# A decoder layer on one core: the order of the instructions on four engines from the first load to the last slot

## Time and profile before

| what | us |
|---|---|
| median of 3 runs | 340.77 (340.64 to 340.9) |
| the profiled execution's own time | 340.39 |
| its span, first to last instruction | 338.6 |
| TensorE matmuls busy | 281.4 |
| VectorE busy | 225.5 |
| ScalarE busy | 229.3 |
| GpSimd busy | 192.3 |

### The profile page before, as it was taken

How to read it: one execution, slowest core, us unless ns; L and a number is a source line. 1 busy time by engine, 2 the same in 40 slices (tenths; PEclk the granted TensorE clock), 3 DMA queues, 4 the chain that set the end, 5 groups by cost and what they waited for, 6 DMA issues and landing times.

```text
span 338.6 us, 5747 instructions
## 1 busy us (share of the span) xinstructions
PE 281.4 (83%) x1518; PEld 213.2 (63%) x1518; DVE 225.5 (67%) x488; ACT 229.3 (68%) x456; POOL 192.3 (57%) x381
## 2 busy tenths in 40 slices
PE   1366747586689899999999999899999999999950
PEld 1253524244366587777878877667888888878740
DVE  2789999999897869977686777363533454443420
ACT  3788788899578759987787787466454564544740
POOL 2436775768847656865755746647425343255571
PEclk9999787859599999999999999999999999999995
DMA  7999981978492792004002202303211021010000
GB/s 241 389 387 387 225 196 62 180 124 161 127 214 98 127 185 66 1 31 158 0 33 93 66 0 89 100 0 129 91 63 33 32 94 62 3 58 30 24 8 6
DMA packets 17407, 37.02 MB, mean 109 GB/s; under 512 B 1504, under 2 KB 1632, under 8 KB 17377
## 3 DMA queue, kind: packets, MB, share of 16 engines
q0 software_dynamic: 6496, 15.74, 19.5%
q1 hardware_dynamic: 10880, 20.92, 19.2%
HBM read 26.68 MB, written 10.76 MB: 111 GB/s over the span
## 4 chain that ended last, share of the span: by engine, by line
PE 62%; ACT 7%; issue 5%; DVE 5%; POOL 3%; DMA 2%; POOLq 0%; ACTq 0%; DVEq 0%; SPq 0%
PE bank_z L1589 5%; PE bank_y L1589 5%; PE bank_z L1590 5%; PE bank_z L1593 5%; PE bank_y L1590 5%; PE bank_y L1593 5%; PE bank_m L1589 4%; PE bank_m L1593 4%; PE bank_m L1590 4%; PE bank_tr L1558 4%; PE bank_c L1491 3%; PE bank_q L1558 2%; PE bank_a L1491 1%; PE bank_m L1553 1%; PE bank_a L1558 1%
## 5 line engine op out<-in xcount | busy, mean ns | idle before, releaser
L353 POOL TENSOR_TENSOR x<-x,bias_b 128x512 f32<-128x512 f32 x19 | 24.6, 1293 | 25.9 <-PE bank_q L1558 25.8
L1589 PE MATMUL bank_y<-c_hi,h_hi 128*128 x76 | 31.5, 415 | 1.6 <-ACT h_hi L650 1.4
L1589 PE MATMUL bank_m<-f_hi,m_hi 128*128 128x512 f32 x76 | 31.5, 415 | 1.6 <-ACT m_hi L650 1.6
L1589 PE MATMUL bank_z<-c_hi,a_hi 128*128 x76 | 30.8, 406 | 2.1 <-issue 1.4
L358 POOL DMA_INDIRECT out<-r,token_of x19 | 20.2, 1063 | 18.6 <-ACT r L689 11.7
L1590 PE MATMUL bank_m<-f_lo,m_hi 128*128 128x512 f32 x76 | 30.1, 396 | 0.0
L1590 PE MATMUL bank_z<-c_lo,a_hi 128*128 x76 | 30.1, 396 | 0.0
L1590 PE MATMUL bank_y<-c_lo,h_hi 128*128 x76 | 30.1, 396 | 0.0
L313 POOL TENSOR_TENSOR n_d<-n_v,minus_half 128x1 f32<-128x1 f32 (+1 forms) x46 | 27.0, 586 | 3.8
L1090 DVE TENSOR_TENSOR act_z<-bank_z,act_z 128x512 f32<-128x512 f32 x19 | 13.1, 688 | 22.0 <-ACT act_z L664 22.0
L312 POOL TENSOR_SCALAR n_v<-n_dev 128x1 f32<-128x1 f32 (+1 forms) x46 | 8.7, 190 | 33.2 <-ACT rows L669 19.7
(11 more groups left out here) (205 smaller groups left out, 855.4 us busy)
## 6 DMA issues: line engine op xcount, KB each, us to landing
f_sum<-in_factors POOLq DMA_DIRECT2D x7, 1024.0 KB, 9.3
rows<-sorted_rows SPq DMA_DIRECT2D x19, 256.5 KB, 2.7
xs<-in_x SPq DMA_DIRECT2D x8, 512.0 KB, 8.4
c_stage<-in_ctx_t SPq DMA_DIRECT2D x4, 1024.0 KB, 14.3
sorted_rows<-pad_row SPq DMA_DIRECT2D x1, 1539.0 KB, 17.4
w_stage<-in_wf_t SPq DMA_DIRECT2D x1, 1024.0 KB, 8.7
w_stage<-in_wi_t SPq DMA_DIRECT2D x1, 1024.0 KB, 10.9
w_stage<-in_wg_t SPq DMA_DIRECT2D x1, 1024.0 KB, 13.1
```

Of the source, the lines that this page charges most:

```text
L353: pool.tensor_tensor(tile, tile, bias_b[:], ALU.add).then_inc(s.x2b, 1)
L1589: t.matmul(bank[:], hi[:, c, :], w_hi(c), start=(c == 0), stop=False)
```

## The change

Every helper stays as it is, and so does every instruction and SyncE's queue. Only the order of the calls on GpSimd, ScalarE, VectorE and TensorE is another one, from the first instruction to the last slot. On GpSimd `weight_ready(W_F)` comes ahead of `number_slots`, and `add_factor(1)`, `scale_g(0)`, `power_x(2)` ahead of `places`. On VectorE the `low_of_ctx` that stood in pairs stand mostly singly. The diff, without indentation and cut to the parts that are spoken of:

```diff
 power_x(0)
 power_x(1)
 fill_events()
+weight_ready(W_F)
 number_slots()
-weight_ready(W_F)
 weight_ready(W_I)
 open_slots()
 weight_ready(W_G)
-places()
 add_factor(1)
 scale_g(0)
 power_x(2)
+places()
 scale_o(0)
 weight_ready(W_O)
 scale_g(1)
 power_x(3)
+add_factor(2)
 number_rows(0)
 power_1(0)
-add_factor(2)
 pool.wait_ge(s.padded, 16)
 scatter_rows(0)
+add_factor(3)
 scale_o(1)
-add_factor(3)
 scale_g(2)
 power_x(4)
 number_rows(1)
+add_factor(4)
 power_1(1)
-add_factor(4)
 scale_o(2)
 scatter_rows(1)
 scale_g(3)
...
-token_of_row(0)
 scale_o(3)
 quantise_o(3)
+token_of_row(0)
+power_x(6)
 add_factor(6)
+token_of_row(1)
+scale_g(4)
 power_2(0)
-token_of_row(1)
-add_bias(0)
-scale_g(4)
-power_x(6)
+add_factor(7)
+token_of_row(2)
+power_1(3)
 number_rows(3)
-add_factor(7)
-power_1(3)
-token_of_row(2)
 power_2(1)
 scatter_rows(3)
+add_bias(0)
...
 for turn in range(MERGE + 2, N_GROUPS):
     g, p, n = turn, turn - 1, 2 * turn - LEAD
+    scale_o(p)
+    token_of_row(n)
+    quantise_o(p)
+    scale_g(g)
     number_rows(p)
-    scale_o(p)
-    quantise_o(p)
+    power_3(n - 3)
+    add_bias(n - 2)
+    token_of_row(n + 1)
     power_2(n - 1)
-    scale_g(g)
-    token_of_row(n)
-    add_bias(n - 2)
-    power_3(n - 3)
     if is_group(g + 2):
         power_x(g + 2)
-    add_bias(n - 1)
     power_3(n - 2)
-    token_of_row(n + 1)
     store(n - 3)
     power_1(p)
     power_2(n)
     scatter_rows(p)
     store(n - 2)
+    add_bias(n - 1)
...
+store(13)
+token_of_row(15)
 token_of_row(16)
+add_bias(16)
 store(14)
-add_bias(16)
+power_3(15)
 power_2(17)
+store(15)
 token_of_row(17)
-power_3(15)
 power_3(16)
-store(15)
 power_2(18)
 add_bias(17)
 store(16)
 add_bias(18)
 power_3(17)
-token_of_row(18)
 store(17)
 power_3(18)
+token_of_row(18)
 store(18)
...
 weight_sum(W_F)
+x_by_channel(0)
 weight_sum(W_I)
-x_by_channel(0)
+weight_sum(W_G)
 max_row(0)
 weight_ready(W_F)
-weight_sum(W_G)
+weight_ready(W_I)
 weight_sum(W_O)
-weight_ready(W_I)
 tanh_f(0, 0)
+square_x(2, 0)
+weight_ready(W_G)
 forget(0, 0)
-weight_ready(W_G)
+high_of_ctx(0, range(0, 1))
 silu_i(0, 0)
-square_x(2, 0)
 square_g(0, 0)
+tanh_f(0, 1)
+high_of_ctx(0, range(1, 2))
+square_g(0, 1)
+silu_i(0, 1)
+max_row(1)
+square_x(2, 1)
+silu_h(0, 0)
+forget(0, 1)
 x_by_channel(1)
...
 silu_i(3, 1)
-tanh_f(3, 1)
-forget(3, 0)
+x_by_channel(4)
+square_g(3, 1)
 forget(3, 1)
+o_by_channel(2)
 square_x(5, 1)
-square_g(3, 0)
-x_by_channel(4)
-o_by_channel(2)
-square_g(3, 1)
+max_row(4)
...
+    if turn == MERGE + 2:
+        high_of_factors()
     if is_group(g + 1):
         x_by_channel(g + 1)
-    if turn == MERGE + 2:
-        high_of_factors()
-    silu_i(g, 0)
+    high_a(n)
+    if is_group(g + 2):
+        square_x(g + 2, 0)
     square_g(g, 1)
+    silu_i(g, 1)
+    tanh_f(g, 1)
+    high_m(n - 2)
+    square_3(n - 3)
+    if is_group(g + 2):
+        square_x(g + 2, 1)
+    silu_z(n)
+    forget(g, 1)
+    o_by_channel(p)
...
 silu_z(10)
 high_a(11)
 high_h(10)
-square_3(8)
 high_a(12)
 high_m(9)
 silu_z(11)
+square_3(8)
+high_h(11)
+norm_3(8)
 square_2(10)
-norm_3(8)
+high_a(13)
+silu_z(12)
 norm_2(10)
...
 square_2(17)
-high_h(18)
-square_3(15)
+norm_3(15)
+square_3(16)
 norm_2(17)
-square_3(16)
-norm_3(15)
 high_m(17)
 square_2(18)
+norm_2(18)
 norm_3(16)
-norm_2(18)
 high_m(18)
...
+choose()
 max_x(0, 0)
+count_tiles()
+v.tensor_copy(ident_h[:], ident).then_inc(s.ident_h, 1)
 max_x(0, 1)
-choose()
-v.tensor_copy(ident_h[:], ident).then_inc(s.ident_h, 1)
-count_tiles()
+scale_x(0)
 max_x(1, 0)
-scale_x(0)
 max_x(1, 1)
+quantise_x(0)
 scale_x(1)
-quantise_x(0)
 order_slots()
 weight_scale(W_F)
-quantise_x(1)
 round_weights(W_F)
 weight_scale(W_I)
+quantise_x(1)
 round_weights(W_I)
+weight_scale(W_G)
 rescale_f(0, 0)
-weight_scale(W_G)
+round_weights(W_G)
 rescale_f(0, 1)
-round_weights(W_G)
 rescale_i(0, 0)
-find_slots()
 next_fills()
+rescale_i(0, 1)
+weigh_eps()
 max_x(2, 0)
-rescale_i(0, 1)
+max_x(2, 1)
 gate_i(0, 0)
+weight_scale(W_O)
+scans(0, 0)
+gate_i(0, 1)
 dve.wait_ge(s.gw, 16)
...
+find_slots()
 scans(0, 1)
-weight_scale(W_O)
+scale_x(2)
 weigh_g(0, 1)
+rescale_f(1, 0)
+quantise_x(2)
+output(0, 0)
+low_of_ctx([0])
+rescale_i(1, 0)
+rescale_f(1, 1)
...
+scans(1, 0)
+low_of_ctx([2])
+scans(1, 1)
 residual_1(0)
-scans(1, 1)
...
 residual_1(1)
-low_of_ctx([9])
-weigh_g(2, 1)
 rescale_f(3, 0)
+scale_x(4)
 output(2, 0)
+rescale_f(3, 1)
 output(2, 1)
 rescale_i(3, 0)
+low_of_ctx([9])
...
             s.fsplit if n == 0 else None)
 ranks_in_tiles()
-weight_total(W_F)
 pe.wait_ge(s.ident_h, 1)
 transpose_x(0)
+spread_max(0)
+weight_total(W_F)
 weight_total(W_I)
-spread_max(0)
+weight_total(W_G)
 project_f(0)
-weight_total(W_G)
-weight_total(W_O)
 pe.wait_ge(s.xqt, 1)
 transpose_x(1)
 project_i(0)
 project_g(0)
 spread_max(1)
...
 transpose_x(2)
@@ -1664,27 +1666,27 @@
 transpose_o(2)
 project_back(2)
 silu_h_by_token(3)
+transpose_a(0)
 project_f(4)
-transpose_a(0)
 project_i(4)
 up(0)
 project_g(4)
 transpose_h(0)
 pe.wait_ge(s.oqt, 3)
 transpose_x(5)
-spread_max(5)
 pe.wait_ge(s.o, GT * MERGE)
 down(0)
 transpose_a(1)
+spread_max(5)
 pe.wait_ge(s.xqt, 6)
 transpose_o(3)
 up(1)
+project_back(3)
+transpose_h(1)
 pe.wait_ge(s.oqt, 4)
 transpose_m(0)
-transpose_h(1)
-project_back(3)
+down(1)
 transpose_a(2)
-down(1)
 up(2)
...
+    down(n - 1)
     if is_group(g + 1):
         pe.wait_ge(s.tml, n - 2)
         transpose_x(g + 1)
-    down(n - 1)
-    pe.wait_ge(s.xqt, min(g + 2, N_GROUPS))
-    transpose_m(n - 2)
-    if is_group(g + 1):
         spread_max(g + 1)
     transpose_a(n)
     mix(n - 3)
+    pe.wait_ge(s.xqt, min(g + 2, N_GROUPS))
+    transpose_m(n - 2)
     up(n)
     pe.wait_ge(s.tml, n - 1)
     transpose_o(p)
     mix(n - 2)
     transpose_h(n)
-    pe.wait_ge(s.oqt, p + 1)
-    transpose_m(n - 1)
     project_back(p)
     transpose_a(n + 1)
...
+mix(n - 2)
 transpose_m(n - 1)
-mix(n - 2)
 up(n + 1)
 mix(8)
 transpose_a(11)
+transpose_m(9)
 transpose_h(10)
-transpose_m(9)
 up(11)
```

More of the change, by code:

```diff
@@ L837, in _ @@
+                    square_2(n - 1)
+                    silu_h(g, 0)
+                    high_h(n)
+                    square_3(n - 2)
+                    norm_2(n - 1)
                     if is_group(g + 1):
                         max_row(g + 1)
-                    tanh_f(g, 1)
-                    high_a(n)
-                    square_2(n - 1)
-                    if is_group(g + 2):
-                        square_x(g + 2, 0)
-                    forget(g, 0)
-                    high_m(n - 2)
@@ L846, in _ @@
-                    square_3(n - 3)
-                    silu_i(g, 1)
-                    silu_z(n)
-                    if is_group(g + 2):
-                        square_x(g + 2, 1)
-                    norm_2(n - 1)
-                    o_by_channel(p)
-                    silu_h(g, 0)
+                    high_a(n + 1)
                     norm_3(n - 3)
-                    high_h(n)
-                    forget(g, 1)
-                    square_3(n - 2)
+                    square_1(p)
                     high_m(n - 1)
-                    high_a(n + 1)
@@ L879, in _ @@
                 high_m(n - 2)
+                norm_3(n - 3)
+                norm_1(p)
+                high_a(n + 1)
                 norm_2(n - 1)
-                norm_1(p)
                 square_2(n)
-                high_a(n + 1)
+                square_3(n - 2)
                 high_m(n - 1)
-                norm_3(n - 3)
-                square_3(n - 2)
                 norm_2(n)
@@ L1220, in _ @@
                 max_o(0, 0)
-                rescale_i(1, 0)
+                round_weights(W_O)
+                max_o(0, 1)
                 rescale_i(1, 1)
-                rescale_f(1, 1)
-                max_o(0, 1)
-                scale_x(2)
-                quantise_x(2)
-                round_weights(W_O)
-                quantise_o(0)
                 gate_i(1, 0)
                 weigh_g(1, 0)
-                max_x(3, 1)
+                gate_i(1, 1)
                 slot_offsets()
-                low_of_ctx([0])
@@ L1247, in _ @@
+                low_of_ctx(range(3, 5))
+                rescale_i(2, 1)
                 max_o(1, 0)
-                rescale_i(2, 0)
-                low_of_ctx(range(4, 6))
                 max_x(4, 0)
+                low_of_ctx([5])
                 max_o(1, 1)
-                quantise_x(3)
+                gate_i(2, 0)
                 weigh_g(2, 0)
-                rescale_i(2, 1)
+                scans(2, 0)
+                gate_i(2, 1)
+                weigh_g(2, 1)
+                quantise_o(1)
@@ L1326, in _ @@
                     rescale_f(g, 0)
+                    hidden(n - 1)
                     rescale_f(g, 1)
-                    hidden(n - 1)
                     rescale_i(g, 0)
@@ L1716, in _ @@
                     down(n)
+                    pe.wait_ge(s.oqt, p + 1)
+                    transpose_m(n - 1)
                     up(n + 1)
@@ L1766, in _ @@
                 mix(12)
```

(14 more changed lines are left out.)

361 lines of the change are left out of this document (172 added, 189 removed).

## The result

The changed kernel takes 345.23 us (median of 4, 344.58 to 346.44), the one before 340.7 beside it: a ratio of 1.0151, 95% interval 1.0128 to 1.0174. That is 4.5 us slower, where I forecast 341.0 and at most 342.8.

What follows compares the result with a forecast made beforehand. VectorE bounds 24 to 98, TensorE's work most of 98 to 207 and 236.6 to 316, chains 207 to 236.6 and the end. Terms -0.9 + 0.1 - 0.1 + 0.7 - 0.4 + 0.8 = +0.2 us: median 341.0, range 339.0 to 342.8.

Steps and rivals of the forecast that it cites:

- 24 to 98, -0.9: Stretch bound by VectorE: its last low_of_ctx ends 0.9 us sooner; term -0.9 us, bounds -5.6 and +0.5.
- `up(0)` at 97.4: Sign in the new profile: the first product starts at 97.4 and not 98.31.
- GpSimd, 0 us with 0.3 to spare: add_factor(1), scale and power ahead of places end near 34.0, before scale_x(2) wants them: cost 0, bounds 0 and +1.1 us.
- The rule of the shared port pair: By it, places beside quantise_x(2) and the first low_of_ctx would cost VectorE time; by the rows, nothing more.
- The start: 10 to 24: second matrix rounded about 1 us sooner, first projection about 0.4 us later, VectorE 0.8 us ahead at 36.
- 98 to 122, +0.1: From up(0) to the end of up(2): 23.8 us where before took 23.7; term +0.1.
- 122 to 236.6, 0 and -0.1: Three turns keep TensorE full, term 0; in the drain silu_z(8) and hidden(8) come sooner, term -0.1.
- My rival for the turns: Turns stall as transpose_o waits for low_m(n - 2) over bank_q: +2.4 on the sum, 343.4 us; chance 0.12.
- 236.6 to 316, +0.7 and -0.4: up(12) behind down(10) starts at 244.9, +0.7; the 0.44 us gap ahead of 303.18 goes, -0.4.
- the end, +0.8: Swapped norms: norm_3(16) behind norm_2(18), its store and all after it late; +0.8 us, bounds 0 and 1.0.
- the first rival: Early gain is large: half of VectorE's 5.6 us idle ahead of 98 goes (-2.3), 339.6 us; chance 0.27.

Runs made afterwards that it cites:

- early: Kernel before with the new order of all four engines up to the loop of turns, the old one from there: 342.4 us, ratio 1.0061.
- start: Kernel before with the new order in the start alone (VectorE through scans(0, 1)), all that follows old: 339.49 us, ratio 0.9985.
- upto_back2: Kernel before with all engines in the new order up to project_back(2) and residual_1(2), the old order behind: 341.35 us, ratio 1.0039.
- from_back2: Kernel before with the new order only from project_back(2) and residual_1(2) to the loop of turns: 340.06 us, ratio 1.0013.
- early_xr_fill: `early` with GpSimd's add_factor(1) behind power_x(2) and VectorE work moved into three places where it stood still: 341.88 us, ratio 1.0056.
- early_xr: `early` with one GpSimd line moved, add_factor(1) behind power_x(2): 342.28 us, ratio 1.0066.
- loop: Kernel before with the new order in the loop of the three turns alone: 341.82 us, ratio 1.0052.
- tail: Kernel before with the new order behind the drain alone (products up(12) to mix(18), norms, stores): 340.34 us, ratio 1.0017.
- loop_pe: Kernel before with the new order of TensorE alone in the loop of turns: 355.48 us, ratio 1.0458.
- early_again: `early` unchanged, measured once more beside its variants: 342.46 us, ratio 1.0075.

## Why the prediction was wrong

- **24 to 98, -0.9.** This is the step that failed: +2.3 us by `early` (mean of its two series, 98 to 122 included), so about 3 off. "At `output(1, 0)`, near 58, VectorE has done `quantise_x(3)` in addition and is 0.2 sooner" held by half until 52 (42.19 us of work done there, 41.73 before), and then 1.25 us were lost at `project_back(0)`, where I had no wait. What failed is the overlap: I counted how much VectorE had done, and not which work. Between the third rounding and `quantise_o(0)` it now has 24.5 us of work and 1.5 of waiting, in before 21.1 and 0.9; `project_back(0)` came 3.9 us later behind that rounding, and too little was left to fill the time of TensorE's projections. At `project_back(1)` I had 1.0 us lost; VectorE was idle for 1.8 us more than before from 60 to 80. That the loss is made in the middle is shown by `start`, `upto_back2` and `from_back2`; that VectorE's waits alone don't make it, by `early_xr_fill`; which of the moved operations on which engine do stays open.
- **`up(0)` at 97.4.** It started near 101.3. I had also overlooked that `max_o(3, 0)` and `rescale_i(4, 0)` now stand between the last `low_of_ctx` and `low_a(0)`; by `from_back2` that costs little.
- **GpSimd, 0 us with 0.3 to spare.** The factor was added at 31.24 and x_r was ready at 35.53, against my 30.5 and 34.0, and VectorE waited 1.10 us. `early_xr` shows that the wait alone decided nothing. The rule of the shared port pair that the prediction takes from the Trainium skill (SBUF — State Buffer, "Who interferes with whom") agrees with the traces on the side of GpSimd: beside VectorE's rounding of weights at 43.1 the two operations of `scale_o(0)` below took 1.01 and 1.72 us (timeline of after, GpSimd), where in before they took 0.20 and 0.70. But before has the same collision, as I had said, with two other operations of `scale_o(0)` (second list), which took 0.70 and 0.29 in after. It isn't what the order changed.

```profile
43.43 1.01 POOL L277 TENSOR_TENSOR o_v<-o_ms,g_u 128x2 f32<-128x2 f32 x1 [1.95 <-ACT squares L610]
44.52 1.72 POOL L278 TENSOR_TENSOR o_r<-o_v,minus_half 128x2 f32<-128x2 f32 x1
```

```profile
42.89 1.94 POOL L282 TENSOR_TENSOR o_rc<-o_mc,minus_one 128x2 f32<-128x2 f32 x1
44.91 1.20 POOL L284 TENSOR_TENSOR o_q<-o_rc,o_r 128x2 f32<-128x2 f32 x1
```

- **The start.** Right in direction: rounding begins earlier, and `start` is 0.15% faster (interval up to 0.05% slower, so not told from nothing). The page before has VectorE at nine tenths from about 25 us on, and not from 10 as I had read it.
- **98 to 122, +0.1.** Right: 0.2 (lag 3.0 at `up(0)`, 3.2 at `up(2)`).
- **122 to 236.6, 0 and -0.1.** Wrong, +1.8 us by `loop`. The words that failed are "`add_bias(n - 1)` at the end of GpSimd's turn has until the next turn's first `mix`": what stands behind it on its own queue is `scale_o(p)`, which is needed at once. My rival for the turns had another mechanism (bank_q and `low_m(1)`); TensorE waits nowhere for m_lo from 122 to 207 us.
- **236.6 to 316, +0.7 and -0.4; the end, +0.8.** 0.7, -0.9 and 0.9 in the profile of `tail`: right but for 0.5 us; the end is the two norms.
- **The range.** The parts with a known duration came out; the walk over four lists didn't. Its error was 3 us in the first section and 1.8 in the turns, and I gave it 0.8. (Half of the 5.6 us of idle time in the first rival is 2.8 and not 2.3; that moves no bound of the range.)

## What to carry to other kernels

When an order changes, find for each long latency (here 7.3 us from a quantisation to the projection that follows) how much of the busiest engine's work stands inside it, before and after: work that moves ahead of its start makes it start later and leaves the engine less to do inside it. For a line moved to the end of an engine's turn, look at what heads that engine's next turn. And exchange sections of all lists together: four lists that each look movable cost 3 to 25 us when only one was moved.

## What was not expected

The same program ran 70 to 80 us at a granted clock of 0.57 in one profiled execution and 0.75 in another; in before it was 0.75, in `loop_pe`, with the same list up to there, 0.91. What decides it stays open. And the first matrix landed between 7.2 and 9.7 us after its issue in the profiled executions, though its load stands in all kernels at the same place. So the lags read from the first profile are softer than they look: `up(0)` began at 101.68 us in `early` and at 98.03 in `early_again`, and in the nine kernels whose lists up to the loop are those of before it began anywhere from 95.7 to 99.3. Counted from ScalarE's first weight sum these nine agree better, 85.7 to 87.9 us, and the changed kernel has 90.0. A lag read across the whole first section of one execution is good to some 2 us either way here; a stretch inside it, from one operation of the same list to another, to about 1.
